# Value bias of the first attention: a one-row matmul per token tile in the value products, in place of GpSimd's addition to the input

## What is computed

```python
attn = softmax(where(causal, phi @ phi.T * T / temp, -inf))
V = x @ W_v.T + b_v
out = attn @ V
return out @ W_out.T + b_out
```

## Time and profile before

| | |
|---|---|
| median of 3 runs | 3010.41 us (3004.92 to 3012.23) |
| the profiled execution | 3010.78 us, span 3008.8 us |
| mean granted TensorE clock | 0.867 of full |
| busy, share of the span | PE 76%, PEld 61%, DVE 72%, ACT 35%, POOL 19% |
| chain that ended last | issue 38%, PE 23%, DVE 18%, DMA 11%, ACT 5%, POOL 4% |

### The profile page before, as it was taken

How to read it: one execution, slowest core, us unless ns; L and a number is a source line. 1 busy time by engine, 2 the same in 40 slices (tenths; PEclk the granted TensorE clock), 3 DMA queues, 4 the chain that set the end, 5 groups by cost and what they waited for, 6 DMA issues and landing times.

```text
span 3008.8 us, 50636 instructions
## 1 busy us (share of the span) xinstructions
PE 2276.8 (76%) x17470; PEld 1830.6 (61%) x17470; DVE 2175.1 (72%) x4246; ACT 1060.2 (35%) x2004; POOL 585.9 (19%) x666
## 2 busy tenths in 40 slices
PE   3667788868776877886877687888677777888875
PEld 3556666657465756664755565666565566666663
DVE  6765788866866578885776667888586666788767
ACT  2312444422432244442242224444224223444324
POOL 2111222212101122221101112222120102222220
PEclk8778899989777889998877789999877878999988
DMA  6001689840001078983000119897100014899600
GB/s 234 1 15 40 137 160 171 154 86 1 1 15 56 15 149 161 170 152 63 1 1 15 56 37 167 166 164 144 31 1 15 1 55 85 161 169 166 113 1 14
DMA packets 658407, 251.39 MB, mean 84 GB/s; under 512 B 613082, under 2 KB 633946, under 8 KB 657370
## 3 DMA queue, kind: packets, MB, share of 16 engines
q1 hardware_dynamic: 653978, 243.79, 41.4%
q10 hardware_dynamic: 4160, 4.19, 0.4%
HBM read 52.87 MB, written 10.49 MB: 21 GB/s over the span
## 4 chain that ended last, share of the span: by engine, by line
issue 38%; PE 23%; DVE 18%; DMA 11%; ACT 5%; POOL 4%; DVEq 1%; ACTq 0%; SPq 0%; POOLq 0%
DMA l_ptb<-l_phb 6%; PE ps L233 5%; PE ps L235 5%; PE ps L234 4%; DMA l_pts<-l_phs 4%; DVE nmax L1385 3%; PE ps L1289 1%; DVE l_k L1440 1%; DVE l_q L1444 1%; DVE l_phb L1391 1%; DVE l_phs L1391 1%; ACT l_q L1351 1%; PE ps L1271 1%; ACT xn L1347 1%; POOL d_pn L990 1%
## 5 line engine op out<-in xcount | busy, mean ns | idle before, releaser
L1385 DVE TENSOR_REDUCE nmax<-ps 128x1 f32<-128x1024 f32 (+7 forms) x512 | 383.3, 750 | 23.0 <-PE ps L1273 20.9
L1494 POOL CAST l_phb<-l_pb 128x1024 f16<-128x1024 f32 (+3 forms) x256 | 241.4, 943 | 654.1 <-ACT l_pb L1336 337.8
L1336 ACT ACTIVATE l_pb<-ps,nmax 128x1024 f32<-128x1024 f32 (+3 forms) x256 | 244.7, 956 | 283.5 <-DVE nmax L1385 282.7
L1271 PE MATMUL ps<-l_k,l_q 128*128 128x512 f32 (+3 forms) x768 | 319.1, 416 | 24.3 <-ACT l_ps L1336 23.9
L1391 DVE TENSOR_TENSOR l_phb<-l_pb,l_phb 128x1024 f16<-128x1024 f32 (+3 forms) x256 | 288.2, 1126 | 15.5 <-POOL l_phb L1494 13.4
L1272 PE MATMUL ps<-l_k,l_q 128*128 128x512 f32 (+3 forms) x768 | 270.1, 363 | 0.0
L1289 PE MATMUL ps<-l_v,l_ptb 128*128 128x64 f16 x4992 | 197.8, 197 | 34.2 <-DMA l_ptb<-l_phb 34.1
L1289 PEld LDWEIGHTS ps<-l_v,l_ptb 128*128 128x128 f16 x4992 | 177.1, 101 | 67.4 <-DMA l_ptb<-l_phb 41.1
L233 PE MATMUL ps<-xTh,l_w 128*128 128x512 f32 x256 | 123.1, 481 | 83.9 <-DVE l_q L1444 50.5
L1494 POOL CAST l_phs<-l_ps 128x128 f16<-128x128 f32 (+3 forms) x256 | 124.2, 485 | 319.1 <-DMA l_pts<-l_phs 169.6
L1271 PEld LDWEIGHTS ps<-l_k,l_q 128*128 128x128 f32 x768 | 156.0, 203 | 44.2 <-ACT l_ps L1336 29.8
(11 more groups left out here) (361 smaller groups left out, 6279.4 us busy)
## 6 DMA issues: line engine op xcount, KB each, us to landing
l_k<-xn SPq DMA_DIRECT2D x128, 256.0 KB, 4.1
l_w<-l_wqk_s SPq DMA_DIRECT2D x32, 512.0 KB, 4.8
l_wv<-l_wv_s SPq DMA_DIRECT2D x16, 512.0 KB, 6.0
xin<-in_x SPq DMA_DIRECT2D x4, 1024.0 KB, 5.5
m_w<-in_m_w SPq DMA_DIRECT2D x8, 512.0 KB, 4.4
m_w<-in_m_w SPq DMA_DIRECT2D x4, 1024.0 KB, 9.2
l_wo<-in_l_wo SPq DMA_DIRECT2D x16, 256.0 KB, 4.5
l_ptb<-l_phb SPq DMA_TRANSPOSE x256, 4.1
```

What stands on the lines that cost most here:

```text
L1271: pe.matmul(s[:, c0:c1], q, L["l_k1"][:, h, c0:c1], start=True, stop=False)
L1336: s.activation(l_numer(k)[:, 0:n], l_banks(k)[:, 0:n], ACT.Exp, bias=nmax[:, k % 4:k % 4 + 1], accum_out=lsum[:, h, k % NT:k % NT + 1]).th ...
L1385: v.tensor_reduce(nmax[:, k % 4:k % 4 + 1], l_banks(k)[:, 0:n], AX.X, ALU.max, negate=True).then_inc(q_["max"], 1)
L1494: g.tensor_copy(l_parts(k)[:, 0:cols], l_numer(k)[:, 0:cols]).then_inc(q_["hi"], 1)
```

## The change

A seventh matmul ends the sum of each value tile: the first row of `ones_f` (1 x 128) times the first row of `bvo` (1 x 256), both plain fp32, adds `bvo` to all 128 token rows. GpSimd's addition goes, with its wait and its count, and the remaining waits on `s_xb` count three additions per item.

```diff
@@ f_pe_value
                 for c in range(DC):
-                    last = mm3(pe, o, xTh[:, c, tok], xTl[:, c, tok], wvo_h[:, c, :], wvo_l[:, c, :], c == 0, c == DC - 1)
+                    mm3(pe, o, xTh[:, c, tok], xTl[:, c, tok], wvo_h[:, c, :], wvo_l[:, c, :], c == 0, False)
+                last = pe.matmul(o, ones_f[0:1, :], bvo[0:1, :], start=False, stop=True)
             last.then_inc(a_sem["v"], 1)
@@ f_g
             x_diagonal_first(g, b)
-            g.wait_ge(s_xn, b * (NPH * NT) + NT)
-            g.tensor_tensor(xin[:], xin[:], bvo[:].unsqueeze(1).to_broadcast([P, NT, D]), ALU.add).then_inc(s_xb, 1)
@@ finish
                 if k == 0:
-                    v.wait_ge(s_xb, b * 4 + 1)
                     v.wait_ge(s_out, b * 16 + 16)
@@ x_v
-                    v.wait_ge(s_xb, b * 4 + (2 if cr is C0 else 4))
+                    v.wait_ge(s_xb, b * 3 + (1 if cr is C0 else 3))
@@ m_v_expert
-            v.wait_ge(s_xb, b * 4 + 3)
+            v.wait_ge(s_xb, b * 3 + 2)
```

## The result

| | before | after |
|---|---|---|
| median of 4 runs | 3011.32 us (3004.92 to 3018.29) | 3071.04 us (3068.84 to 3075.3) |
| the profiled execution, its span | 3010.78, 3008.8 us | 3072.29, 3070.5 us |
| mean granted TensorE clock | 0.867 | 0.855 |

A forecast was written before the change was run, and what follows sets the result against it. No engine was taken as full; chains of handovers between PE, ACT, DVE and DMAs bound the kernel. Item 0's -1.0 plus 3 x (2.8 + 0.4) gave +8.6 us on 3010.4, so 3019.0 us, range 3008 to 3029.

The forecast's parts named there:

- The sign: Whole kernel: the change was forecast to make it slower, by 8.6 us or 0.29%.
- the two sources: A gain of 4.35 us on DVE from L714's removal, against the cost of 32 bias matmuls added on PE.
- the places: Gain in item 0 at L670 and L668; added matmul time in value steps t = 5 and t = 7.
- step t = 7: Value groups 2 and 3, items 1 to 3: four bias matmuls on PE's path, 2.8 us per item, bounds 1.6 to 5.0.
- step t = 5: Value groups 0 and 1, items 1 to 3: added work mostly absorbed by gaps, 0.4 us per item, bounds 0 to 1.5.
- The gain: DVE in item 0: L670 and L668 shorten without L714, together 4.35 us; nothing in items 1 to 3.
- The price of a bias matmul: Each added matmul on PE: 0.7 us at full clock (bounds 0.41 to 0.95), 1.25 us at half clock.
- Item 0: First item: L839 comes 3.4 us late, less the 4.35 us gain, net -1.0 us; about -3 if cheap, +1 if dear.
- The clock rises later: Rival: one-row matmuls delay the rise in step t = 7 past value group 3; 3032 us, 0.17 shared with dear depth changes.
- The clock kept: Rival: bias matmuls fill PE's gaps, 2.4 GHz holds in two items, giving back 8 us; 3011 us, chance 0.20.
- The matmul is cheap: Rival: depth changes are hidden, step t = 7 costs 1.6 us per item, item 0 gains 3; 3012 us, chance 0.13.
- the stall moves: Rival: L670 in item 0 is long for another reason than L714, 4.35 us stay; 3023 us, folded into the upper end.

The follow-up runs named there:

- f3_adjacent: Changed kernel with each group's second tile taking its bias first, so two one-row matmuls stand side by side; 3047.84 us, 1.0102 of the kernel before.

## Why the prediction was wrong

The sign, the two sources and the places were right. The size was not: 8.6 us forecast, 57 measured, far outside the range. The step that failed is the pricing of the added work at the clock of before, 2.8 us for step t = 7 and 0.4 us for step t = 5 in each of items 1 to 3; at the half clock that the changed kernel in fact had, they measured 8.7 and 7.2. By its own steps:

- **The gain** was put at 4.35 us in item 0. L670 gave its 4.14. The 0.21 for L668 was wrong, since L669 takes 0.63 us without L714 too. Nothing in items 1 to 3, as forecast: the kernel with the removal alone has their fronts within 0.9 us.
- **The price of a bias matmul** was put at 0.7 us in full clock and 1.25 in half. At half clock it is 1.45: 0.85 of streaming and 0.60 for the change of depth, where the earlier trace rows had been read as 0.41. The reading was sound in kind, but it charged one change where the matmul has two; two at that price, 0.82 + 2 x 0.41 = 1.64, would have held the truth, and the bound that was used at half clock, 1.25, did not. The trace of before has a nearer reading, where the combinations, 64 rows deep, give way to value group 2 at 841.23:

```profile
840.84 0.47 PE L235 MATMUL ps<-wc_h,a_phl 64*128 64x320 f32 x1
...
841.61 0.41 PE L234 MATMUL ps<-wvo_l,xTh 128*128 128x256 f32 x1
```

From L235 to L233 it is 0.39 us where the combinations step by 0.27, and from there to L234 0.38 where the products step by 0.21. That is 0.29 us for one change of depth at half clock, so 0.58 for two, which is the surcharge measured later. At full clock the changed kernel's own matmuls in these steps don't show it; the pair of f3_adjacent in item 0 leaves about 0.4 for the excursion, so 0.43 + 0.4 = 0.83 is an estimate.

- **Step t = 7** is where the first large error lies. "If it rises at the same moment, the added work is in effect done at full clock: 4 x 0.7 = 2.8 us." It didn't rise at all in this step, and the stretch took 10.91 us where 6.9 were forecast. The four matmuls cost 4 x 1.45 = 5.8 us, the twelve products behind the former rise another 1.0, which makes the measured 6.83, and L781 1.8 more in front of ACT's copy: 8.7 where 2.8 were forecast.
- **Step t = 5** was put at 0.4 us and cost 7.2. The sentence that failed is "some 2 if the clock rises within them" together with the 1.4 for group 1, which assumed full clock behind the rise as in before. Group 1 ran at half instead: 2 x 1.45 for its bias matmuls and some 1.1 for its products. The 0.76 us gap was filled as forecast, but DVE's L1654 came to wait 5.54 us, and the combinations behind it, at half clock, added 1.5. I had set 3.4 us of added work against three gaps, while in truth the added time up to the end of group 1 was nearly 7 us and the gaps absorbed about 1 of it.
- **Item 0** was put at -1.0 and is +11.3, for the same reason: half clock from the first value product to 127 us.
- **The rivals.** "The clock rises later" named the mechanism, with 3032 us and a part of 0.17. It too let the clock fall back into its old course behind group 3, and gave step t = 5 only 1.5 us. "The clock kept" had it the wrong way round: the one-row matmuls filled the gaps in PE's record, as it said, and the clock was lower all the same. The prediction had drawn on the Trainium skill's "TensorE: Matmul & The Clock Gate", section "HAM oscillation — how this bites in real kernels", where gaps in PE's work let the clock fall. The trace doesn't bear out the use it made of that: 33.78 us of 34 are recorded busy, at 0.50. The section's own case is a wait for DMA between bursts of matmuls, far longer than the gaps of 0.76, 1.16 and 0.45 us here, so this trace doesn't contradict the section itself. "The matmul is cheap" and "the stall moves" fell with the measured 1.45 and with L671.

What the two errors share is that I took the clock of before as given, though the trace had it rise twice within these 25 us. A sequence that sits on such an edge should have had the forecast "half clock all the way" worked out in full: 8 x 1.45 us, 1.1 + 1.0 for the products, 1.5 for the combinations, 1.8 for `x_pe_m`, less about 1 of gaps. That comes to 16 per item, and to 15.8 in the trace; the 1.45 is measured afterwards, and with the prediction's own 1.25 it would have been 14.4.

**What is shown and what stays open.** Shown: the loss is in the matmuls, not in the removal; it goes away when the same matmuls have the depth of their neighbours, and at that depth more streaming costs little beyond its own time. With fewer rows, their number makes no difference clear of the intervals, while the fp32r pair halves the loss, pairs of one-row matmuls leave about half of it, and eight columns a third. Open: by what the clock is held down. Fewer excursions and less one-row streaming each left a higher clock in some stretch, so both may take part. The pauses of about 0.6 us at the excursions, which PE's own rows don't record as idle, are a guess at the cause; no run paused PE for the same time at constant depth, so that isn't shown. Open too is most of the gain of the full-depth fp32r form. Its fronts sum to -0.4 us, and the rest of its 8 us isn't located: the parts of the program outside the fronts differ by 11.5 us between the two profiled executions of this very kernel, and by up to 22 us among all of them. That is why the fronts, and not the profiled totals, carry the comparisons above.

## What to carry to other kernels

A rank-one or few-row matmul set between full-depth ones isn't free filler. Give it the depth of its neighbours, with the identity and a bias that stands in all rows, and compare the two forms by the starts of the records around it, not by their durations. Where the trace of before shows the granted clock rising and falling inside the stretch to be edited, work out the sum once with the lower clock for the whole stretch, for the unchanged matmuls too. Before an operation is moved to another engine to rid a third one of a stall, try moving it in time: the one-line later wait removed the same 4.14 us stall with nothing added on PE, though a gain of that size lies at the edge of what the ratio shows here.

## What the runs showed of the hardware that I had not expected

- An excursion from 128 rows to fewer and back costs 0.59 to 0.60 us at 1.2 GHz, read from three comparisons, and it is the same with 1, 32 and 64 rows, and once for two neighbours. A single change from 64 to 128 rows in the kernel before costs 0.29. With fp32 and eight columns the whole matmul costs 0.81 us.
- Across such a change no weight load runs ahead of its matmul: PEld is idle for 0.22 and 0.65 us around the one-row matmul, and no idle time is recorded around the full-depth one.
- PE recorded as busy in 33.78 of 34 us, at half clock throughout. Here busy time in the record was no sign that the clock would rise.
- The same 48 matmuls with the same gaps ran at 0.50 in one execution and at 0.83 in another, 13.22 against 8.94 us.
